# Two-layer transformer on one core: second layer's turn placed behind the q/k projection, other PSUM banks for second heads, and a last stage that alternates by head

## The chip, the cores and the metric

The kernel runs on one core of one Trainium2 chip. The metric is the device time of one execution in microseconds; lower is better. Before the change it is 988.21 us (median of 3 runs, 987.48 to 988.67).

## The reference

Eight sequences (B = 8) of 256 tokens with 256 features pass through two layers. Layer 0 has 16 attention heads of 128 dimensions with a causal mask, beside a feed-forward block in fp8. Layer 1 has 16 heads of 16 dimensions without a mask, beside a gated feed-forward block with Hadamard transforms.

```python
x = L0_attn_query                      # (8, 256, 256)
xn = _layernorm(x)
x = x + attn0(xn) + ffn0(xn)           # 16 heads x 128, causal, f32; fp8 feed-forward
xn = _layernorm(x)
x = x + attn1(xn) + ffn1(xn)           # 16 heads x 16, no mask; silu(gate) * up, then down
# attention: softmax(q @ k.T * scale) @ v, then @ w_o + b_o
```

## The kernel before, in words

Every f32 product is made of three bf16 products. A value is split into a high part (ScalarE copies PSUM to bf16) and a low part (VectorE subtracts the high part from PSUM). So nearly each PSUM tile is read first by ScalarE (`..._high`, line 807 or 808) and then by VectorE (`..._low`, line 812 or 813), and its bank is free only after both. There are eight banks: BK_QK, BK_M, BK_S, BK_O, BK_X, BK_VU, BK_S1, BK_Y.

The work is a software pipeline of steps s, written out as one list for each engine. The engines keep to their lists in order and meet through semaphores. The first stage of the kernel (layer 0's feed-forward, to about 110 us) is not touched. In steps 0 to 127 (NG0 = 128) a step does, on PE: `scores0(s-1)` (layer 0's scores, bank BK_S), the layer-1 scores of the head that belongs to the step (`scores1`, BK_S1), the q/k projection `proj_qk0(s)` (BK_QK), `turn0(s-2)` (the transposes of layer 0's softmax weights, BK_S again), `project_out0(s-4)` (BK_X), `turn1` (the transposes of the layer-1 weights of the head of step s-1, BK_O), then `proj_v0` in even steps or `up_gate` in odd ones (BK_VU), at some steps layer-1 pieces (`transpose_x1`, `proj_qkv1`, `attend1`: BK_M; `down`, `project_out1`: BK_Y), and last `attend0(s-3)` (BK_O). These names are functions of the kernel. Most matmuls are recorded at line 819 (the helper `group`); others have their own lines: `turn0` 841, `turn1` 869, `scores1` 902, `project_out0` 941, `attend1` 953, `transpose_x1` 965, `attend0` 1040 and 1042, `down` 1058, `project_out1` 1069. On the other engines: `max_0` 1321, `max_1` 1328 and the reciprocals 1350 and 1354 on VectorE; both exponentials 1162 and `gate_tanh` 1238 on ScalarE; `hidden` 1399 to 1406 on VectorE; the normalisations 1552 and 1559 and `hidden_low` 1564 on GpSimd.

A layer-1 sequence b starts 16 (b + 1) steps in (`start1`). Its heads lie one to a step from step 28 to 123 (sequences 0 to 5). The seventh sequence (b = 6) puts most of its 16 heads two to a step, into steps 124 to 132, and the eighth (LASTB = 7), which has no layer-0 work beside it, puts two into each of the steps from END = 134 to 141. The second head of a step is told by `second(n)`. Before, its scores go to BK_M and its turned weights to BK_S1. `x1_sum`, the layer norm, `transpose_x1(7)` and `proj_qkv1` (BK_S, BK_O, BK_X for the eighth sequence) lie in steps 131 to 133.

The waits that matter here: `turn1` into BK_O waits until `o0_low(s-4)` has emptied that bank; `attend0(s-3)`, which writes BK_O too, waits for `p1_low` of the head just turned and for `p0_low` of its own; `scores0(s)` at the start of the next step waits for `qk0_low(s)` and for `p0_low(s-2)`, since it writes BK_S. ScalarE's list of a step is `o0_high`, `exp_0`, `o1_high`, `qk0_high`, `p0_high`, `p1_high`, `exp_1`, then `v0_high` or `gate_tanh`. VectorE's is `max_0`, `o0_low`, `max_1`, `o1_low`, the reciprocal, `qk0_low`, `p0_low`, `p1_low`, second heads' `max_1`, `rec_1`, then `v0_low` or `hidden`. For steps from 134 on there is a shorter list for each engine. No DMA and no list of the DMA queue changes.

Of the kernel before, what the change touches and what calls it, by code (L numbers as in the profile page):

```python
# [18 lines left out]
def build(nc, t):  # L19
# [17 lines left out]
    with ExitStack() as ctx:  # L37
# [649 lines left out]
        def score1_bank(n):  # L687
            b, h = divmod(n, H1)
            if b == LASTB:
                return (BK_S1, BK_S)[h % 2]  # L690
            return BK_M if second(n) else BK_S1

        def turn1_bank(n):

            if n < LASTB * H1:
                return BK_S1 if second(n) else BK_O
            if n % 2 == 0:
                return BK_O
            return BK_X if head_slot(n) + 1 < END + 3 else BK_Y

        def second(n):

            return n > 0 and head_slot(n) == head_slot(n - 1)
# [112 lines left out]
        def pe_program(pe):  # L816
# [28 lines left out]
            def turn1(n):  # L845
                bank, slot = turn1_bank(n), head_slot(n) + 1
                if n < B * H1 - 1:
                    pe.wait_ge(norm1, n + 1)
                else:
                    pe.wait_ge(norm_last, 1)  # L850
                before = [m for m in range(n) if turn1_bank(m) == bank]
                if before:
                    pe.wait_ge(p1_lo, before[-1] + 1)
                if bank == BK_QK:
                    pe.wait_ge(qk0_lo, min(slot + 1, NG0))
                elif bank == BK_S1:
                    pe.wait_ge(exp1, 1 + max(m for m in range(B * H1)
                                             if score1_bank(m) == BK_S1 and head_slot(m) <= slot))
                elif bank == BK_X or bank == BK_O and n >= LASTB * H1:
                    pe.wait_ge(qkv1_lo, 3 * B)  # L860
                elif bank == BK_O:
                    pe.wait_ge(o0_lo, min(slot - 3, NG0))
                    if slot >= piece_slot(3 * LASTB):
                        pe.wait_ge(qkv1_lo, 3 * LASTB + 2)
                else:
                    pe.wait_ge(y_done, LASTB)
                for k in range(TT):
                    for i in range(TT):
                        last = nc.tensor.transpose(ps[:, bank, k * T + i * P:k * T + (i + 1) * P],  # L869
                                                   p1_of(n)[:, i, k * P:(k + 1) * P], ident[:, :])  # L870
                last.then_inc(p1_ps, 1)

            def scores1(n):
# [16 lines left out]
                    pe.wait_ge(p1_lo, turned[-1] + 1)  # L890
                if bank == BK_M:
                    free_m(pe, 0, n)
                if b == LASTB:
                    m, r = divmod(h // 2, 4)
                    rows32 = slice(32 * r, 32 * r + 32)
                    for i in range(TT):
                        last = group(ps[:, bank, i * T:(i + 1) * T],
                                     [(qm[rows32, h % 2, a, m, i * P:(i + 1) * P], qk1[rows32, c, 1, m, :])
                                      for a, c in PARTS])
                else:  # L900
                    for i in range(TT):
                        last = nc.tensor.matmul(ps[:, bank, i * T:(i + 1) * T],  # L902
                                                qs[:, h // 2, h % 2, i * P:(i + 1) * P],
                                                ks[:, b % 2, h // 2, :], start=True, stop=True)
                last.then_inc(s1_ps, 1)

            def proj_qk0(n):
                b, g = divmod(n, H0)
                if n == 0:
                    pe.wait_ge(xT_lo, PAIRS)  # L910
                if g == 0 and b >= 2:
                    pe.wait_ge(cur_ready[b % 2], 16 * (b // 2))
                if b == 0 and g % 4 == 0:
                    weights_ready(pe, ("qk", g // 4))
                for w in range(2):
                    last = group(ps[:, BK_QK, w * T:(w + 1) * T],
                                 [(wqkv0[:, a, w, k, g * HD0:(g + 1) * HD0], cur[:, b % 2, c, k, :])
                                  for k in range(KD) for a, c in PARTS])
                last.then_inc(qk0_ps, 1)
# [176 lines left out]
            for s in range(END):  # L1096
# [13 lines left out]
                for n in heads_in[s]:  # L1110
                    if second(n):
                        scores1(n)
                if 0 <= s - 2 < NG0:
                    turn0(s - 2)
                if 0 <= s - 4 < NG0:
                    project_out0(s - 4)
                for n in heads_in[s - 1]:
                    if not second(n):
                        turn1(n)
                if v_in(s) is not None:  # L1120
                    proj_v0(v_in(s))
                for n in hidden_in[s]:
# [20 lines left out]
                    pe_linear0(pe, PAIRS - 1, s - 4)  # L1143

            for s in range(END, y_slot(LASTB)):
                for n in heads_in[s]:
                    scores1(n)
                for n in heads_in[s - 1]:
                    turn1(n)
                for n in hidden_in[s]:  # L1150
                    up_gate(n, s)
                for n in downs_in[s]:
                    down(n)
                for n in outs_in[s]:
                    project_out1(n)
                for n in quads_in[s]:
                    attend1(n)

        def act_program(act):
# [91 lines left out]
            for s in range(END):  # L1251
# [9 lines left out]
                    exp_0(s - 1)  # L1261
                for n in quads_in[s - 1]:
                    o1_high(n)
                if s < NG0:
                    qk0_high(s)
                if 0 <= s - 2 < NG0:
                    p0_high(s - 2)
                for c in splits_in[s]:
                    split_high(act, c, 0)
                for n in heads_in[s - 1]:  # L1270
                    if not second(n):
                        p1_high(n)
                for n in heads_in[s]:
                    exp_1(n)
                if v_in(s) is not None:
# [19 lines left out]
            for s in range(END, y_slot(LASTB)):  # L1295
                for n in quads_in[s - 1]:
                    o1_high(n)
                for n in hidden_in[s - 1]:
                    gate_tanh(n)
                for e in range(2):  # L1300
                    for n in heads_in[s - 1][e:e + 1]:
                        p1_high(n)
                    for n in heads_in[s][e:e + 1]:
                        exp_1(n)

        def dve_program(dve):
            def o0_low(n):
# [153 lines left out]
            for s in range(END):  # L1461
# [27 lines left out]
                        o1_low(n)  # L1489
                if 0 <= s - 1 < NG0:  # L1490
                    rec_0(s - 1)
                if s < NG0:
                    qk0_low(s)
                if 0 <= s - 2 < NG0:
                    p0_low(s - 2)
                for n in heads_in[s - 1]:
                    if not second(n):
                        p1_low(n)
                fold(s)
                for n in heads_in[s]:  # L1500
                    if second(n):
# [27 lines left out]
            for s in range(END, y_slot(LASTB) + 1):  # L1529
                for n in quads_in[s - 1]:  # L1530
                    o1_low(n)
                for e in range(2):
                    for n in heads_in[s][e:e + 1]:
                        max_1(n)
                    for n in heads_in[s - 1][e:e + 1]:
                        p1_low(n)
                    if e == 0:
                        for n in hidden_in[s - 1]:
                            hidden(n)
                    for n in heads_in[s][e:e + 1]:  # L1540
                        rec_1(n)
                if B * H1 - 1 in heads_in[s]:
                    norm_1(B * H1 - 1)
                for b in y_in[s]:
# [246 lines left out]
```

## Time and profile before

| what | value |
|---|---|
| median of 3 runs | 988.21 us |
| the profiled execution | 989.46 us |
| its span, first to last instruction | 987.5 us |
| mean granted TensorE clock | 0.978 |
| PE busy | 905.1 us (92%) |
| VectorE busy | 753.9 us (76%) |
| ScalarE busy | 680.5 us (69%) |
| GpSimd busy | 347.0 us (35%) |

Span is the time from the first to the last instruction of the program in that one execution. Busy time is the union of an engine's instructions. Matmuls overlap each other, so PE's busy time includes the tail of each; start-to-start distances tell better what PE does in a step. A wait is put down to the instruction that released it last.

### The profile page before, as it was taken

What the parts mean: (1) busy time and instruction counts of PE and PEld (TensorE: products, weight loads), DVE (VectorE), ACT (ScalarE), POOL (GpSimd) and SP (SyncE); (2) the same over time, 40 slices, a digit from 0 to 9 for tenths busy, and PEclk for the clock granted to TensorE, in tenths of its full rate; (3) what the DMA queues carried; (4) which work ended last, traced back from release to release, by engine and by line L of the source; (5) the groups of instructions that cost most, each with busy time, mean ns of one, the idle gap of its engine ahead of it and who ended that gap; (6) DMA issues with size and microseconds to landing.
All of it is one profiled execution on the core that took longest, in us unless ns stands there. A gap on an engine that the chain in (4) does not pass through costs nothing.

```text
span 987.5 us, 22866 instructions
## 1 busy us (share of the span) xinstructions
PE 905.1 (92%) x8032; PEld 724.6 (73%) x8032; DVE 753.9 (76%) x2128; ACT 680.5 (69%) x1997; POOL 347.0 (35%) x637
## 2 busy tenths in 40 slices
PE   4786889899999999999999999999999999886887
PEld 2344667677788788887888788888888888765665
DVE  6886677667887888888888878788888888766466
ACT  4786786557767776777677777777677767755454
POOL 5502456424333333333333333333333333333242
PEclk9998999999999999999999999999999999989799
DMA  9243260002000100010002000200020001000000
GB/s 309 78 150 96 91 209 2 2 22 60 2 2 23 48 23 2 23 50 23 1 3 70 1 23 2 66 7 23 2 62 10 23 2 39 22 23 1 2 12 12
DMA packets 46880, 39.98 MB, mean 40 GB/s; under 512 B 4400, under 2 KB 42032, under 8 KB 46512
## 3 DMA queue, kind: packets, MB, share of 16 engines
q1 hardware_dynamic: 46768, 38.52, 12.7%
q8 instruction: 66, 1.08, 0.5%
q14 instruction: 46, 0.38, 0.1%
HBM read 30.11 MB, written 8.39 MB: 39 GB/s over the span
## 4 chain that ended last, share of the span: by engine, by line
PE 60%; DVE 18%; ACT 10%; issue 4%; ACTq 0%; DVEq 0%
PE ps L819 32%; PE ps L941 6%; ACT arena L1162 5%; DVE arena L812 5%; PE ps L869 5%; DVE arena L813 4%; PE ps L1040 3%; PE ps L1058 3%; PE ps L841 3%; ACT arena L808 3%; DVE arena L1321 3%; PE ps L902 2%; ACT arena L807 2%; PE ps L1069 2%; PE ps L1042 1%
## 5 line engine op out<-in xcount | busy, mean ns | idle before, releaser
L813 DVE SCALAR_TENSOR_TENSOR arena<-ps,bqk,arena 128x256 bf16<-128x256 f32 x416 | 187.5, 480 | 77.0 <-ACT arena L808 77.0
L808 ACT ACTIVATE arena<-ps,bqk 128x256 bf16<-128x256 f32 x416 | 177.8, 463 | 82.4 <-PE ps L1042 64.0
L812 DVE TENSOR_TENSOR arena<-ps,arena 128x512 bf16<-128x512 f32 (+1 forms) x336 | 204.4, 633 | 35.3 <-ACT arena L807 35.0
L819 PE MATMUL ps<-arena,wqkv 128*128 128x256 bf16 x1728 | 216.9, 276 | 0.3 <-DVE arena L812 0.3
L807 ACT ACTIVATE arena<-ps 128x512 bf16<-128x512 f32 (+1 forms) x336 | 181.0, 558 | 47.6 <-PE ps L869 30.3
L1552 POOL TENSOR_SCALAR arena<-arena,rc 128x128 f32<-128x128 f32 (+1 forms) x256 | 105.5, 425 | 273.2 <-DVE rc L1350 273.1
L1162 ACT ACTIVATE arena<-arena,nb 128x128 f32<-128x128 f32 (+1 forms) x256 | 114.4, 447 | 126.3 <-DVE nb L1321 126.2
L1559 POOL TENSOR_SCALAR arena<-arena,rc 128x256 f32<-128x256 f32 x254 | 118.2, 478 | 232.1 <-DVE rc L1354 232.1
L819 PEld LDWEIGHTS ps<-arena,wqkv 128*128 128x128 bf16 x1728 | 171.5, 99 | 24.5 <-issue 0.8
L1162 ACT ACTIVATE arena<-ps,nb 128x256 f32<-128x256 f32 x256 | 119.3, 478 | 16.3 <-DVE nb L1328 16.3
L819 PE MATMUL ps<-arena 128*128 128x128 bf16 (+2 forms) x864 | 98.4, 251 | 16.7 <-DVE arena L813 6.5
L941 PE MATMUL ps<-wo,arena 128*128 128x256 bf16 x768 | 105.4, 274 | 0.9 <-DVE arena L813 0.9
L819 PE MATMUL ps<-wqkv,arena 128*128 128x512 bf16 (+1 forms) x480 | 105.7, 359 | 0.0
L1321 DVE CUSTOM_DVE_ANT_0 arena<-ps,mask 128x128 f32<-128x128 f32 (+1 forms) x256 | 81.0, 354 | 31.2 <-PE ps L819 30.9
L819 PE MATMUL ps<-arena,wug 128*128 128x256 bf16 x768 | 95.6, 275 | 0.0
L1328 DVE TENSOR_REDUCE nb<-ps 128x2 f32<-128x512 f32 x128 | 87.1, 680 | 0.5 <-PE ps L819 0.4
L869 PE MATMUL ps<-ident,arena 128*128 128x128 f32 x512 | 78.4, 279 | 9.3 <-ACT arena L1162 7.2
L819 PEld LDWEIGHTS ps<-arena,wug 128*128 128x128 bf16 x768 | 75.7, 99 | 8.8 <-issue 0.2
L941 PEld LDWEIGHTS ps<-wo,arena 128*128 128x128 bf16 x768 | 74.4, 98 | 10.0 <-DVE arena L813 1.1
L819 PEld LDWEIGHTS ps<-arena 128*128 128x128 bf16 (+1 forms) x864 | 62.4, 98 | 26.3 <-DVE arena L813 14.8
L869 PEld LDWEIGHTS ps<-ident,arena 128*128 128x128 f32 x512 | 60.2, 143 | 15.1 <-issue 11.6
L819 PEld LDWEIGHTS ps<-wqkv,arena 128*128 128x128 bf16 x480 | 47.2, 98 | 32.7 <-issue 0.8
(115 smaller groups left out, 1283.6 us busy)
## 6 DMA issues: line engine op xcount, KB each, us to landing
scratch_qk<-arena SPq DMA_DIRECT2D x28, 128.0 KB, 1.9
arena<-scratch_qk SPq DMA_DIRECT2D x84, 32.0 KB, 1.8
arena<-scratch_qk SPq DMA_DIRECT2D x42, 64.0 KB, 2.5
arena<-in_x SPq DMA_DIRECT2D x4, 512.0 KB, 9.7
arena<-in_w_gating SPq DMA_DIRECT2D x4, 512.0 KB, 7.7
arena<-in_w_q SPq DMA_DIRECT2D x4, 512.0 KB, 4.6
arena<-in_w_k SPq DMA_DIRECT2D x4, 512.0 KB, 5.6
arena<-in_w_v SPq DMA_DIRECT2D x2, 1024.0 KB, 6.5
```

The costliest lines, as they stand in the source:

```text
L807: return nc.scalar.activation(out, in_, ACT.Copy)
L808: return nc.scalar.activation(out, in_, ACT.Identity, bias=bias)
L812: return nc.vector.tensor_tensor(out, in_, hi, ALU.subtract)
L813: return nc.vector.scalar_tensor_tensor(out=out, in0=in_, scalar=bias, in1=hi, op0=ALU.add, op1=ALU.subtract)
L819: last = nc.tensor.matmul(out, lhsT, rhs, start=(n == 0), stop=(n == len(steps) - 1))
L869: last = nc.tensor.transpose(ps[:, bank, k * T + i * P:k * T + (i + 1) * P], p1_of(n)[:, i, k * P:(k + 1) * P], ident[:, :])
L941: last = nc.tensor.matmul(ps[:, BK_X, i * D:(i + 1) * D], oT0[:, a, n % 2, i * P:(i + 1) * P], wo0[:, c, h, :], start=False, stop=(h == H0 ...
L1162: last = nc.scalar.activation(outs[i], ins[i], ACT.Exp, bias=bias[:, i:i + 1], scale=scale, accum_out=sums[:, i:i + 1])
L1321: last = nc.vector.tensor_tensor_reduce(out=sp0[:, n % 3, a:z], in0=ps[:, BK_S, a:z], in1=mask[:, a:z], scale=-SCALE0, scalar=3.0e38, op0= ...
L1328: nc.vector.tensor_reduce(nb1[:, n % 4, :], ps[:, score1_bank(n), :].rearrange("p (i k) -> p i k", i=TT), AX.X, ALU.max, negate=True).then ...
L1552: last = nc.gpsimd.tensor_scalar(v, v, rc0[:, n % 4, i:i + 1], 1.0, ALU.mult, ALU.mult)
L1559: last = nc.gpsimd.tensor_scalar(v, v, rc1[:, n % 4, i:i + 1], 1.0, ALU.mult, ALU.mult)
```

## The change

Three things change, with no instruction added or removed.

1. `turn1` of a step's first head comes directly behind `proj_qk0` (and a second head's scores), ahead of `turn0` and `project_out0`, on PE; `p1_high` stands ahead of `qk0_high` on ScalarE; `p1_low` ahead of `qk0_low` and `p0_low` on VectorE.
2. Second heads use other banks. Scores go to BK_M in steps up to 127 and to BK_QK from 128. Turned weights go to BK_QK in steps up to 127 and to BK_S from 129. The waits follow the banks; `proj_qk0` gains one, for a turn in BK_QK.
3. In steps from 134 on PE does the first head's scores and turn, `up_gate`, and then the second head's scores and turn. ScalarE's `gate_tanh` and VectorE's `hidden` lie between the two heads.

```diff
@@ score1_bank, turn1_bank
-            return BK_M if second(n) else BK_S1
+            if second(n):
+                return BK_M if head_slot(n) < NG0 else BK_QK
+            return BK_S1
...
-                return BK_S1 if second(n) else BK_O
+                if second(n):
+                    return BK_QK if head_slot(n) + 1 < NG0 else BK_S
+                return BK_O
@@ turn1, scores1, proj_qk0: waits
-                elif bank == BK_S1:
-                    pe.wait_ge(exp1, 1 + max(m for m in range(B * H1)
-                                             if score1_bank(m) == BK_S1 and head_slot(m) <= slot))
+                elif bank == BK_S:
+                    pe.wait_ge(p0_lo, NG0)
...
+                if bank == BK_QK:
+                    pe.wait_ge(qk0_lo, NG0)
...
+                turned = [m for m in range(B * H1) if turn1_bank(m) == BK_QK and head_slot(m) + 1 < n]
+                if turned:
+                    pe.wait_ge(p1_lo, turned[-1] + 1)
@@ PE, steps below END
+                for n in heads_in[s - 1]:
+                    if not second(n):
+                        turn1(n)
                 if 0 <= s - 2 < NG0:
                     turn0(s - 2)
                 if 0 <= s - 4 < NG0:
                     project_out0(s - 4)
-                for n in heads_in[s - 1]:
-                    if not second(n):
-                        turn1(n)
@@ PE, steps from END
-                for n in heads_in[s]:
-                    scores1(n)
-                for n in heads_in[s - 1]:
-                    turn1(n)
-                for n in hidden_in[s]:
-                    up_gate(n, s)
+                for e in range(2):
+                    for n in heads_in[s][e:e + 1]:
+                        scores1(n)
+                    for n in heads_in[s - 1][e:e + 1]:
+                        turn1(n)
+                    if e == 0:
+                        for n in hidden_in[s]:
+                            up_gate(n, s)
@@ ScalarE, steps below END
+                for n in heads_in[s - 1]:
+                    if not second(n):
+                        p1_high(n)
                 if s < NG0:
                     qk0_high(s)
                 if 0 <= s - 2 < NG0:
                     p0_high(s - 2)
                 for c in splits_in[s]:
                     split_high(act, c, 0)
-                for n in heads_in[s - 1]:
-                    if not second(n):
-                        p1_high(n)
@@ ScalarE, steps from END
-                for n in hidden_in[s - 1]:
-                    gate_tanh(n)
                 for e in range(2):
                     for n in heads_in[s - 1][e:e + 1]:
                         p1_high(n)
                     for n in heads_in[s][e:e + 1]:
                         exp_1(n)
+                    if e == 0:
+                        for n in hidden_in[s - 1]:
+                            gate_tanh(n)
@@ VectorE, steps below END
+                for n in heads_in[s - 1]:
+                    if not second(n):
+                        p1_low(n)
                 if s < NG0:
                     qk0_low(s)
                 if 0 <= s - 2 < NG0:
                     p0_low(s - 2)
-                for n in heads_in[s - 1]:
-                    if not second(n):
-                        p1_low(n)
@@ VectorE, steps from END
                     for n in heads_in[s - 1][e:e + 1]:
                         p1_low(n)
+                    for n in heads_in[s][e:e + 1]:
+                        rec_1(n)
                     if e == 0:
                         for n in hidden_in[s - 1]:
                             hidden(n)
-                    for n in heads_in[s][e:e + 1]:
-                        rec_1(n)
```

## Rows read from the trace of the kernel before

**Rows 1.** Busy time by stretch, two of fifty us: PE, PEld, DVE, ACT, POOL, then PEclk, DMA share, GB/s

```profile
500.00:550.00 50.00, 49.22 (x468) 41.41 (x467) 40.03 (x114) 36.99 (x115) 16.53 (x36) 1.00 0.13 36
...
850.00:900.00 50.00, 40.54 (x348) 31.83 (x344) 34.19 (x95) 32.61 (x104) 17.17 (x37) 0.93 0.04 12
```

**Rows 2.** Waits of PE from 250 to 850 us: us in total, times, longest

```profile
PE ps L1040 <- DVE arena L812: 6.8, 18, 0.5
PE ps L841 <- DVE nb L1321: 2.7, 6, 0.5
```

**Rows 3.** Timeline of step 92, and the same `attend0` one round (16 steps) later

```profile
646.90 0.48 DVE L813 SCALAR_TENSOR_TENSOR arena<-ps,bqk,arena 128x256 bf16<-128x256 f32 x1
...
647.43 0.49 PE L841 MATMUL ps<-ident,arena 128*128 128x128 f32 x3
...
648.41 0.60 PE L869 MATMUL ps<-ident,arena 128*128 128x128 f32 x4
648.62 1.02 ACT L807 ACTIVATE arena<-ps 128x384 bf16<-128x384 f32 x2
...
648.76 0.88 DVE L813 SCALAR_TENSOR_TENSOR arena<-ps,bqk,arena 128x256 bf16<-128x256 f32 x2 [0.56 <-ACT arena L808]
...
649.55 1.15 DVE L812 TENSOR_TENSOR arena<-ps,arena 128x384 bf16<-128x384 f32 x2
...
650.84 0.49 PE L1040 MATMUL ps<-arena 128*128 128x256 bf16 x3 [0.53 <-DVE arena L812]
...
651.33 0.33 PE L819 MATMUL ps<-arena 128*128 128x128 bf16 x3
...
753.05 0.49 PE L1040 MATMUL ps<-arena 128*128 128x256 bf16 x3 [0.53 <-DVE arena L812]
```

**Rows 4.** Waits of PE from 850 us to the end: us in total, times, longest

```profile
PE ps L869 <- ACT arena L1162: 7.2, 7, 3.4
PE ps L819 <- ACT arena L1162: 3.5, 5, 1.7
PE ps L902 <- DVE arena L812: 3.3, 4, 1.8
PE ps L902 <- DVE arena L813: 3.0, 2, 2.1
```

**Rows 5.** Timeline of steps 128 to 133, where PE waits longest

```profile
885.66 0.58 PE L902 MATMUL ps<-arena 128*128 128x256 bf16 x2 [2.08 <-DVE arena L813]
...
913.86 1.09 PE L869 MATMUL ps<-ident,arena 128*128 128x128 f32 x4 [3.36 <-ACT arena L1162]
...
920.37 1.08 PE L869 MATMUL ps<-ident,arena 128*128 128x128 f32 x4 [1.69 <-ACT arena L1162]
...
923.07 0.80 PE L819 MATMUL ps<-arena,wqkv 128*128 128x256 bf16 x3 [0.34 <-DVE arena L812]
```

**Rows 6.** Busy time of one stretch, columns as in the first group

```profile
912.80:926.40 13.60, 10.39 (x46) 7.28 (x47) 5.70 (x12) 5.70 (x18) 3.52 (x8) 0.50 0.01 1
```

**Rows 7.** Timeline of one round of the last sequence (steps 140 and 141)

```profile
966.75 0.82 PE L819 MATMUL ps<-arena 32*128 32x256 bf16 x6 [0.50 <-ACT arena L1162]
...
967.50 1.12 PE L869 MATMUL ps<-ident,arena 128*128 128x128 f32 x8
...
969.43 0.41 DVE L1399 SCALAR_TENSOR_TENSOR arena<-arena,ps 128x256 f32<-128x256 f32 x1
...
970.62 0.67 DVE L1328 TENSOR_REDUCE nb<-ps 128x2 f32<-128x512 f32 x1
...
971.32 0.47 ACT L1162 ACTIVATE arena<-ps,nb 128x256 f32<-128x256 f32 x1 [1.13 <-DVE nb L1328]
...
972.24 0.38 ACT L1238 ACTIVATE arena<-ps 128x256 f32<-128x256 f32 x1
...
972.40 0.82 PE L819 MATMUL ps<-arena 32*128 32x256 bf16 x6 [0.40 <-ACT arena L1162]
```

## The prediction

> **What bounds the kernel now.** I read four views in this order: busy time by stretch, the waits of PE, the timeline of a step, and the timeline of the end. The stretch from 500 to 550 us has PE busy for 49.2 of 50 us at the full granted clock (1.00, the 2.4 GHz level); from 850 us it falls to 40.5 of 50 [rows 1]. So up to step 123 PE is the bound, and behind it nobody is. In 250 to 850 us PE's named waits are only 6.8 us ahead of `attend0` (L1040) and 2.7 us ahead of `turn0` (L841) [rows 2]. These rows understate a little, since a matmul's own tail counts as busy; counted from start to start I find about 2.75 us lost in each 16 steps. One round of 16 steps is 753.05 - 650.84 = 102.2 us (the same `attend0` of two rounds) [rows 3].
>
> The last two sequences are different: between 850 us and the end PE waits 7.2 us ahead of `turn1` (L869) for an exponential, and 3.3 and 3.0 us ahead of `scores1` (L902) for VectorE's conversions, besides 3.5 us ahead of the last sequence's scores [rows 4]. Nearly all of these are waits for a PSUM bank, not for data.
>
> **The middle (steps 28 to 123, six rounds).** `turn1` moves ahead of `turn0` and `project_out0`; `p1_high` and `p1_low` move ahead of the q/k and p0 conversions. No instruction is added. Take the step whose rows are shown [rows 3]. Before, `turn1` starts at 648.41, ScalarE's copy ends at 649.64, but `p1_low` stands behind `p0_low` and ends at 649.55 + 1.15 = 650.70; `attend0`, which writes the same bank, starts 0.14 us after that. That 0.14 is the hand-off VectorE to PE. The bank BK_O is also why the moved `turn1` gets a new neighbour: it needs `o0_low`, which ends at 646.90 + 0.48 = 647.38, so it can start at 647.52, not at 647.43 where `turn0` starts now. From there: 1.23 us to the end of the copy (648.41 to 649.64), 0.03 and 0.69 for `p1_low`: 649.47, 1.2 us earlier, and the wait at `attend0` is gone.
>
> What is late next: the q/k and p0 conversions. They end about 3.3 us after `turn1`'s start (1.23 for the copy, about 0.8 for ScalarE's q/k pair, 0.88 for VectorE's [rows 3], 0.5 for p0, less overlaps), so at 650.83, and the next step's `scores0`, which reuses BK_S, can start at 650.97. Before it starts at 651.33 [rows 3]: 0.36 us won. But ScalarE now waits for `turn1` early, and behind that wait stand its q/k, p0, exp, v and tanh work, behind `p1_low` those of VectorE: the last conversions of a step end 0.1 to 0.2 us later (an estimate from the same rows); VectorE begins the next step late, `o0_low` is late, and the new `turn1` stands right behind it. Going so through the 16 positions of a round, I win 0.37, 0.32, 0.13 and 0.14 us (positions 12, 15, 14, 10, counted as step number modulo 16) and lose 0.43, 0.09, 0.08, 0.07, 0.04 (positions 0, 4, 13, 9, 5); the rest have no wait before or after. Sum -0.25 us a round, **-1.5 us** for six. Bounds: all waits go, -2.75 x 6 = -16 us; or the positions that lose do so twice as much and those that win do not, +0.7 x 2 x 6 = +8 us. I take -1.5 as the one worked out from the rows, nearer the middle of the two.
>
> The Trainium skill ("Trainium Kernel Development and Optimization", Performance Expectations) says that matmul busy time is a bad metric because matmuls are pipelined. By it the round has more to give than the busy rows show; my count from start to start agrees in direction, 2.75 us a round against 1.6 (9.5 us of named waits in some six rounds). The sum above already uses the larger figure as its bound; by the smaller one the bound would be -9.5.
>
> **Steps 124 to 133, two heads a step.** Here the second head's turn wrote BK_S1, so it waited for this step's exponential and held up the next step's scores; its scores wrote BK_M, which the quads and pieces of the second layer use. The change puts turns into BK_QK (steps 125 to 127) and BK_S (from 129), and scores into BK_QK from step 128.
> - Steps 124 to 127: scores still use BK_M, and the turn in BK_QK now needs this step's `qk0_low` and holds up the next `proj_qk0` until `p1_low`. That comes out at the same time as before within 0.1 us twice. About -0.2 us in all.
> - Step 128: PE waits 2.08 us before 885.66 for `o1_low` (BK_M) [rows 5]. In BK_QK it only needs the last `p1_low`, about 883.2. With `turn1` early, VectorE's second maximum comes some 2.9 us earlier; step 129 starts 3.3 us earlier.
> - Steps 129 to 131: `scores1` no longer waits for a turn in BK_S1 (the wait of at most 1.8 us in [rows 4]); now `o0_low` behind `hidden` is what turn1 waits for. Gain grows to 4.5 us at `x1_sum`.
> - Steps 131 and 132: the waits of 3.36 us before 913.86 and of 1.69 us before 920.37 [rows 5] are for an exponential of the same bank. In BK_S they go; what remains is VectorE's and GpSimd's own chain (layer norm, maximum, reciprocal, norm, turn). The last sequence's q projection, now at 923.07 [rows 5], starts about 6.9 us earlier.
> The ceiling is the three bank waits, 7.2 + 3.3 + 3.0 = 13.5 us; the floor is nothing, if VectorE's chain holds all. I take **-6.9**, about half, the value of the walk.
>
> **The end (steps 134 to 141).** The scores are K = 32 rows and each step's two heads went in pairs. A round now is 972.40 - 966.75 = 5.65 us [rows 7]: scores of the odd head, the turns at 967.50 behind them, copy, `p1_low`, the hidden conversion 969.43 to 970.62, the odd maximum, the exponential at 971.32, and 1.08 us later the next odd scores. After the change the even turn does not stand behind the odd scores, so that ring is cut. The next ring is on VectorE and ScalarE: maximum 0.67, exponential with hand-off 1.08 less 0.1, tanh 0.38, hidden with reciprocal 1.19, maximum 0.67, exponential 0.98, reciprocal 0.15: 5.0 us. PE's own work in a step is about 4.8, so it is close behind. Six rounds at 0.6 are 3.6; the first step and the drain add about 0.4: **-4.0 us**, bounds 0 (if ScalarE's new order, tanh behind the even exponential, holds `hidden` up) and -5.6 (PE's 4.8 alone, with the first step).
>
> **The clock.** From 912.8 to 926.4 us the granted clock is 0.50, the 1.2 GHz level, after a stretch in which PE was idle for 3.36 us in one piece [rows 5, 6]; the q/k/v projection of the last sequence runs in it at half speed. I keep it as it is: even after the change PE waits there for the layer norm. If it vanished, some 3 us more would go. The Trainium skill ("TensorE: Matmul & The Clock Gate", HAM oscillation) says idle gaps bring the half rate and sustained work lifts it; by that rule the shorter gaps could give back these 3 us. The trace agrees so far that the low level follows idle PE.
>
> **Sum.** -1.5 - 0.2 - 6.9 - 4.0 = -12.6, and the -0.2 is already within the -6.9, so -12.4. The profiled execution took 989.46 us (span 987.5), 1.25 above the median of 988.21; against the median the result is 988.21 - 12.4 = **975.8 us**.
>
> **The rivals.**
> - *The middle wins all of its waits*: the ring over VectorE is shorter than I reckon and PE runs without a gap. -16 - 11 = -27: 961 us. For: the rows show hand-offs of 0.14 only. Against: five of 16 positions start VectorE late already. 0.07.
> - *The tail's banks were not the bound*: layer norm, maxima and conversions take the time the bank waits had; 6.9 becomes 2, and the end gives 2. 988.2 - 5.5 = 982.7. For: VectorE is busy in much of it. Against: in both large waits the exponential waited for is followed by nothing that PE needs but the bank. 0.14.
> - *Slower, by `turn1` behind `o0_low`*: place: the middle, 96 steps. The margin is small: `o0_low` ends 0.05 us ahead of the projection's successor in [rows 3] and 0.3 in most steps, the hand-off costs 0.14. If VectorE's later end carries over, each step grows, and all three engines run in one ring. At 0.2 us a step this is +19 - 11 = +8: 996 us. It decides at 11 / 96 = 0.115 us a step; my walk has five positions beyond this, but not the mean. 0.09.
> - *The clock returns* (above): 972.5. 0.06.
> - *No difference*, middle and tail cancelling within 2 us: 0.03.
> Nothing in the order of semaphores keeps the change from doing what it says.
>
> **How the numbers follow.** The forecast has 0.61. Its own range is 970 to 981 from the bounds of its terms (the middle -5 to +3, the tail 2 either way). The range for 8 in 10 reaches to the rival at 982.7 and the clock's, so 966 to 984.5; outside remain the two extreme rivals and no change. A measurement tells about 0.2%, 2 us. Faster: 0.61 + 0.07 + 0.14 + 0.06 = 0.88. Same 0.03. Slower 0.09.
>
> **What would show it.** In the middle: no wait left ahead of L1040, new waits ahead of L869 (for L813) and of the first L819 of a step (for L812), a round of 102.0. At step 128 no wait for `o1_low`; the q projection of the last sequence at about 915 us; rounds of 5.0 at the end. Wrong would be: a round above 103 or below 100 us, or the last exponentials still 5.6 us apart.

## The result: 0.5% faster, a third of the forecast gain

| | before | after |
|---|---|---|
| median | 988.40 us (6 runs, 987.30 to 989.13) | 984.14 us (6 runs, 982.89 to 985.07) |
| profiled execution, span | 989.46, 987.5 us | 984.19, 982.1 us |
| mean granted clock | 0.978 | 0.984 |

The ratio is 0.9949, its 95% interval 0.9933 to 0.9964. Forecast were 975.8 us, -12.4; measured are -4.3 in the medians and -5.4 in the spans. The time lies inside the stated range, at its upper end.

I took the two timelines apart at the same six places in each: the first `scores0` of steps 26 and 124, the last sequence's q projection, its first scores (head 112), its last exponential (head 127) and the final result; the last two stages stand together below. Differences of those start times:

| stage, us | before | after | change | forecast |
|---|---|---|---|---|
| start to step 26 | 226.7 | 228.0 | +1.3 | 0 |
| steps 26 to 123 | 623.15 | 625.12 | +1.97 | -1.5 |
| step 124 to the last q projection | 73.23 | 66.62 | -6.6 | -6.9 |
| that projection to the first scores | 8.2 | 8.9 | +0.6 | 0 |
| the end, with its drain | 53.0 | 50.3 | -2.7 | -4.0 |

**Steady state.** Waits of PE from 250 to 850 us in the changed kernel, which answer to [rows 2].

```profile
PE ps L872 <- DVE arena L817: 10.2, 19, 0.8
```

Busy time in the stretches of [rows 1], columns as there.

```profile
500.00:550.00 50.00, 49.43 (x468) 42.09 (x470) 40.62 (x117) 36.96 (x115) 15.90 (x34) 1.00 0.13 36
...
850.00:900.00 50.00, 40.89 (x380) 33.18 (x380) 36.98 (x103) 34.69 (x112) 18.08 (x39) 1.00 0.04 13
```

The 6.8 us ahead of `attend0` are gone, as forecast, and so are the 2.7 ahead of `turn0`. In their place is a single wait: `turn1` (L872 now) for `o0_low` (a conversion at L817), 10.2 us in 19 waits. The waits were swapped for one of about the same total, 10.2 us for 9.5. PE's busy share says nothing about that: it rose from 49.22 to 49.43 of 50 us while the middle got longer. The second wait that I had named, of a step's first `scores0` for L816, is not in the view.

**Step 80, the worst of each round (position 0).** The timeline of PE and VectorE in the kernel before:

```profile
566.87 0.66 PE L819 MATMUL ps<-arena 128*128 128x128 bf16 x6
566.98 0.41 DVE L1399 SCALAR_TENSOR_TENSOR arena<-arena,ps 128x256 f32<-128x256 f32 x1
...
568.64 0.48 DVE L813 SCALAR_TENSOR_TENSOR arena<-ps,bqk,arena 128x256 bf16<-128x256 f32 x1
...
568.90 0.49 PE L841 MATMUL ps<-ident,arena 128*128 128x128 f32 x3
...
571.61 0.38 PE L823 MATMUL ps<-brow,ones 128*128 128x512 bf16 x1
571.83 0.82 PE L1058 MATMUL ps<-wdn,arena 128*128 128x256 bf16 x6
```

And the same step in the changed kernel:

```profile
568.49 0.66 PE L823 MATMUL ps<-arena 128*128 128x128 bf16 x6
...
569.01 0.41 DVE L1410 SCALAR_TENSOR_TENSOR arena<-arena,ps 128x256 f32<-128x256 f32 x1
...
570.33 0.42 DVE L1332 CUSTOM_DVE_ANT_0 arena<-ps,mask 128x256 f32<-128x256 f32 x1
...
570.67 0.48 DVE L817 SCALAR_TENSOR_TENSOR arena<-ps,bqk,arena 128x256 bf16<-128x256 f32 x1
...
571.29 0.63 PE L872 MATMUL ps<-ident,arena 128*128 128x128 f32 x4 [0.63 <-DVE arena L817]
571.76 0.49 PE L845 MATMUL ps<-ident,arena 128*128 128x128 f32 x3
571.96 0.60 ACT L811 ACTIVATE arena<-ps 128x512 bf16<-128x512 f32 x1 [0.18 <-PE ps L872]
```

Count from the step's first `scores0`. PE reached its turn 2.03 us in (568.90 - 566.87) and `o0_low` ended 2.25 us in; that cost nothing, because `turn0`, which came first, does not wait for it. Now VectorE starts its `hidden` work 0.52 us in instead of 0.11, `o0_low` ends 2.66 us in, and `turn1`, which does use BK_O, stands there until 2.80. `turn0` stands behind it. It needs only `max_0`, whose second half (L1332) ended at 570.33 + 0.42 = 570.75, and with the 0.14 us that VectorE to PE took in [rows 3] it could have started 2.40 us in. So two things come together here: everything on VectorE is late, and `turn1` is at the head of the list. The out projection is no loser of its own, since it waits for the same `o0_low`.

**The tail and its clock.** The timeline of PE in steps 128 to 132 of the changed kernel, which answers to [rows 5].

```profile
886.63 0.38 PE L907 MATMUL ps<-arena 128*128 128x256 bf16 x2 [0.39 <-issue]
...
912.57 0.66 PE L973 MATMUL ps<-ident,arena 128*128 128x128 f32 x4 [2.53 <-DVE arena L1441]
...
914.87 2.29 PE L872 MATMUL ps<-ident,arena 128*128 128x128 f32 x8 [1.43 <-POOL arena L1570]
...
919.70 0.58 PE L823 MATMUL ps<-arena,wqkv 128*128 128x256 bf16 x2 [1.25 <-DVE arena L816]
```

Busy time of the stretch that answers to [rows 6].

```profile
913.70:923.90 10.20, 7.69 (x34) 5.25 (x35) 4.17 (x11) 4.94 (x14) 2.81 (x6) 0.52 0.01 2
```

The waits of 2.08, 3.36 and 1.69 us are gone. What is left are waits for the layer norm (L1441) and GpSimd's norm (L1570), and ahead of them `turn1` behind `o0_low` again, as forecast for steps 129 to 131 (L872 for L817 in the view below, 6.9 us from step 124 on). Behind the 2.53 us of idle PE the granted clock is again at its 1.2 GHz level (0.52).

**The end.** Waits of PE from 850 us on in the changed kernel, which answer to [rows 4].

```profile
PE ps L872 <- DVE arena L817: 6.9, 6, 1.8
PE ps L823 <- DVE arena L816: 2.6, 2, 1.3
PE ps L973 <- DVE arena L1441: 2.5, 1, 2.5
PE ps L872 <- DVE arena L1346: 2.1, 1, 2.1
```

Timeline of one round of the last sequence, which answers to [rows 7].

```profile
960.87 0.47 ACT L1172 ACTIVATE arena<-ps,nb 128x256 f32<-128x256 f32 x1 [1.38 <-DVE nb L1339]
961.79 0.47 ACT L812 ACTIVATE arena<-ps,bv 128x256 bf16<-128x256 f32 x1
962.29 0.48 DVE L817 SCALAR_TENSOR_TENSOR arena<-ps,bv,arena 128x256 bf16<-128x256 f32 x1 [0.20 <-ACT arena L812]
962.69 0.68 DVE L1339 TENSOR_REDUCE nb<-ps 128x2 f32<-128x512 f32 x1
...
966.58 0.47 ACT L1172 ACTIVATE arena<-ps,nb 128x256 f32<-128x256 f32 x1 [1.38 <-DVE nb L1339]
```

In the last four rounds odd exponentials come 5.0 and 5.7 us apart by turns. The 5.71 (960.87 to 966.58) is a step with `o1_high` (L812) and `o1_low` (L817), which stand first in the lists. All seven distances between the odd exponentials of the last sequence:

| into step | 135 | 136 | 137 | 138 | 139 | 140 | 141 |
|---|---|---|---|---|---|---|---|
| before | 7.14 | 5.65 | 5.65 | 6.87 | 5.65 | 5.65 | 5.65 |
| after | 6.89 | 5.31 | 5.65 | 5.70 | 5.01 | 5.71 | 5.00 |

The 6.87 stands out. Up to its start the kernel before ran at the 1.2 GHz level for 3.4 us, and one `up_gate` (the matmuls from wug) took 2.73 us instead of 1.47. PE's timeline, and busy time of the stretch with columns as in [rows 1]:

```profile
948.58 0.82 PE L819 MATMUL ps<-arena 32*128 32x256 bf16 x6 [1.71 <-ACT arena L1162]
...
950.29 2.73 PE L819 MATMUL ps<-arena,wug 128*128 128x256 bf16 x12
...
957.13 1.47 PE L819 MATMUL ps<-arena,wug 128*128 128x256 bf16 x12
```

```profile
950.30:953.70 3.40, 3.40 (x18) 2.25 (x16) 2.97 (x7) 2.27 (x9) 1.02 (x3) 0.50 0.25 80
```

The changed kernel has no such stretch between its last sequence's first scores and last exponential. So of the 2.7 us won at the end some 1.2 (6.87 - 5.65) come with the clock and some 1.4 with the order; this is an estimate from the distances above, since every profile with the old end has the stretch.

### The profile page after: what moved, and what is told of

Read it like the earlier page. It is cut to its first block, busy times and chain, and to the rows that moved or that the text cites. A ratio compares the mean times of both kernels' runs of the same rounds, so it can differ in the third digit from the quotient of the medians.

```text
span 982.1 us, 22791 instructions
## 1 busy us (share of the span) xinstructions
PE 895.5 (91%) x7965; PEld 722.1 (74%) x8032; DVE 761.7 (78%) x2128; ACT 682.9 (70%) x1997; POOL 348.3 (35%) x637
## 4 chain that ended last, share of the span: by engine, by line
PE 64%; DVE 17%; ACT 7%; issue 5%; POOL 0%; another core or an unknown queue 0%; ACTq 0%; DVEq 0%; POOLq 0%
PE ps L823 34%; PE ps L949 6%; PE ps L872 6%; DVE arena L817 4%; PE ps L1066 3%; PE ps L845 3%; PE ps L1048 3%; ACT arena L1172 3%; ACT arena L812 3%; DVE arena L816 3%; DVE arena L1332 2%; PE ps L1077 2%; PE ps L907 2%; PE ps L961 2%; PE ps L1050 1%
## 5 line engine op out<-in xcount | busy, mean ns | idle before, releaser
L816 DVE TENSOR_TENSOR arena<-ps,arena 128x512 bf16<-128x512 f32 (+1 forms) x336 | 212.7, 636 | 74.9 <-ACT arena L811 74.2
L812 ACT ACTIVATE arena<-ps,bqk 128x256 bf16<-128x256 f32 x416 | 179.9, 472 | 66.1 <-PE ps L1050 49.5
L823 PE MATMUL ps<-arena,wqkv 128*128 128x256 bf16 x1728 | 216.8, 276 | 2.7 <-DVE arena L816 2.6
L811 ACT ACTIVATE arena<-ps 128x512 bf16<-128x512 f32 (+1 forms) x336 | 187.9, 564 | 43.3 <-PE ps L872 29.8
L817 DVE SCALAR_TENSOR_TENSOR arena<-ps,bqk,arena 128x256 bf16<-128x256 f32 x416 | 187.5, 479 | 34.0 <-ACT arena L812 30.1
L1570 POOL TENSOR_SCALAR arena<-arena,rc 128x256 f32<-128x256 f32 x254 | 119.0, 482 | 232.1 <-DVE rc L1365 232.1
L823 PEld LDWEIGHTS ps<-arena,wqkv 128*128 128x128 bf16 x1728 | 171.2, 99 | 27.1 <-DVE arena L816 2.0
L823 PE MATMUL ps<-arena 128*128 128x128 bf16 (+2 forms) x864 | 98.3, 250 | 14.7 <-DVE arena L817 6.5
L872 PE MATMUL ps<-ident,arena 128*128 128x128 f32 x512 | 80.0, 279 | 21.8 <-DVE arena L817 17.1
L1332 DVE CUSTOM_DVE_ANT_0 arena<-ps,mask 128x128 f32<-128x128 f32 (+1 forms) x256 | 80.8, 353 | 24.1 <-PE ps L823 23.4
L823 PE MATMUL ps<-wqkv,arena 128*128 128x512 bf16 (+1 forms) x425 | 94.0, 357 | 2.8
L823 PE MATMUL ps<-arena,wug 128*128 128x256 bf16 x768 | 94.3, 273 | 0.0
L872 PEld LDWEIGHTS ps<-ident,arena 128*128 128x128 f32 x512 | 56.9, 142 | 37.6 <-issue 26.9
L823 PEld LDWEIGHTS ps<-arena,wug 128*128 128x128 bf16 x768 | 75.1, 98 | 8.8 <-issue 0.2
L823 PEld LDWEIGHTS ps<-arena 128*128 128x128 bf16 (+1 forms) x864 | 61.5, 98 | 26.3 <-DVE arena L817 14.8
L823 PEld LDWEIGHTS ps<-wqkv,arena 128*128 128x128 bf16 x480 | 47.2, 98 | 33.3 <-issue 1.0
```

Source lines behind the costliest of these rows:

```text
L811: return nc.scalar.activation(out, in_, ACT.Copy)
L812: return nc.scalar.activation(out, in_, ACT.Identity, bias=bias)
L816: return nc.vector.tensor_tensor(out, in_, hi, ALU.subtract)
L817: return nc.vector.scalar_tensor_tensor(out=out, in0=in_, scalar=bias, in1=hi, op0=ALU.add, op1=ALU.subtract)
L823: last = nc.tensor.matmul(out, lhsT, rhs, start=(n == 0), stop=(n == len(steps) - 1))
L1332: last = nc.vector.tensor_tensor_reduce(out=sp0[:, n % 3, a:z], in0=ps[:, BK_S, a:z], in1=mask[:, a:z], scale=-SCALE0, scalar=3.0e38, op0= ...
```

## The experiments

Runs that were sent together share the runs of the kernel before on their chip: 988.58 us (27 runs) for e1 to e4, 988.12 (17 runs) for e5, e6, e9 and e11, and 991.65 (11 runs, 987.96 to 992.63) for e7, e12 and e13. The ratio is what compares across these groups.

**e1, the middle alone.** The new order of `turn1` and p1 in steps below 124; banks and end as before.

```diff
+        EARLY = lambda s: s < 124
                 for n in heads_in[s - 1]:
-                    if not second(n):
+                    if not second(n) and EARLY(s):
                         turn1(n)
                 ...
+                for n in heads_in[s - 1]:
+                    if not second(n) and not EARLY(s):
+                        turn1(n)
```

(the same around `p1_high` and `p1_low`)

> Only part 1, and only in steps below 124; banks and the last stage are as before. Theory A (turn1 now stands behind o0_low, and the steps that start late pay more than the removed waits at attend0 give): about 2 us slower than before, a round of 16 steps of 102.55 us instead of 102.22, the loss in positions 0, 4, 5 and 9, waits ahead of L869 for L813 in their place. Rival B (the middle is neutral or better, and the missing gain of the changed kernel is elsewhere, for instance in its first 230 us, where its profile is 1.3 us late): 0 to 1.5 us faster, and a start of step 26 at 226.7 us as before.

Measured: 990.00 us, 12 runs, ratio 1.0021 (1.0009 to 1.0033). Steps 26 to 123 take 625.11 us against 623.15. PE's waits of 250 to 850 us:

```profile
PE ps L870 <- DVE arena L814: 10.2, 19, 0.8
```

That is the same wait as in the changed kernel. The reordering by itself makes the kernel slower, by 2.0 us in the middle; the sign of my term was wrong.

**e2, the banks alone.** The hunks of `score1_bank`, `turn1_bank` and their waits; all lists as before.

> Only part 2 (banks of the second heads); order and last stage as before. Theory A (the bank waits of steps 124 to 133 carry the gain of this stage, and the order is needed for about a third of it): the last sequence's q projection starts 4 to 5 us earlier, 4 to 5 us faster in all. Rival B (the bank waits are covered by VectorE's chain unless turn1 comes early): at most 2 us faster.

Measured: 983.01 us, 10 runs (977.60 to 986.34), ratio 0.9943 (0.9923 to 0.9963); the profiled execution was the slowest of these. Step 124 to the last q projection takes 65.96 us, no more than with the early turns on top (66.62). So the banks carry the gain of that stage without the order. The middle is as before, 623.14 us, and so are PE's waits of 250 to 850 us:

```profile
PE ps L1048 <- DVE arena L816: 7.3, 19, 0.5
PE ps L845 <- DVE nb L1329: 2.7, 6, 0.5
```

**e3, the end alone.** The hunks of the lists from END on PE, ScalarE and VectorE.

> Only part 3 (the last stage alternates by head). Theory A: from the start of the last sequence's scores to the end 2.5 to 3 us are saved, rounds of 5.0 us without and 5.7 us with an o1 conversion, about 2.7 us faster in all. Rival B (half of what the changed kernel gains here is the half-clock stretch at 950 us, which it misses by chance of its timing): 1.2 to 1.5 us faster.

Measured: 987.29 us, 12 runs, ratio 0.9983 (0.9968 to 0.9997). The stage from the first scores of the last sequence to its last exponential takes 43.02 us instead of 45.69, as in the changed kernel (43.03). That is theory A's size, but it doesn't rule out rival B: e3 misses the half-clock stretch of the end too, while e1 and e2, with the old end, have it at the same place (19.0 and 19.3 us behind their first scores, 19.0 before) and take 45.69 us as well. The whole run gained less than the stage, 0.3 to 3.2 us by its interval.

The three parts add up within their intervals, which are 1 to 2 us wide either way: +2.1 - 5.6 - 1.7 = -5.2 us by their ratios, against -5.0 by the ratio of the whole change (0.0051 x 988).

**e4, the change without its middle.** e1's edit with `EARLY = lambda s: s >= 124` on the changed kernel.

> The changed kernel with the old order in steps below 124, the new one from 124. Theory A (the middle costs 2 us): 2 us faster than the changed kernel, 6.3 us faster than the kernel before (982.1). Rival B (the middle costs nothing): the same as the changed kernel, 4.3 us faster than before (984.1).

Measured: 981.46 us, 6 runs, ratio 0.9933 (0.9917 to 0.9950); the middle is back at 623.05 us. The interval of the ratio overlaps that of the whole change, so it is the stage that tells: with e1 it shows from both sides that the middle costs 2 us. PE's waits of 250 to 850 us are those of before:

```profile
PE ps L1049 <- DVE arena L817: 7.2, 19, 0.5
PE ps L846 <- DVE nb L1339: 2.7, 6, 0.5
```

**e5, o1's conversions out of the ring.** The changed kernel, with `o1_high` and `o1_low` behind the first head's p1 conversion in the steps from END.

```diff
-                for n in quads_in[s - 1]:
-                    o1_high(n)
                 for e in range(2):
                     for n in heads_in[s - 1][e:e + 1]:
                         p1_high(n)
+                    if e == 0:
+                        for n in quads_in[s - 1]:
+                            o1_high(n)
```

(and so for `o1_low`, behind `p1_low`)

> The changed kernel; in the last stage the o1 conversions of both engines move from the front of a step to behind the first head's p1 conversion, where both engines wait 0.3 to 0.5 us. Theory A (a round of the last stage is a ring over VectorE and ScalarE, and the o1 conversions lie in it in every other round): the rounds of 5.7 us become 5.0 to 5.2, three of them, 1.5 to 2 us faster than the changed kernel. Rival B (PE's own work of 5.0 us and project_out1 bound those rounds): 0 to 0.3 us.

Measured: 982.62 us, 6 runs, ratio 0.9941 (0.9925 to 0.9957). The last sequence's stage shrinks from 43.03 to 41.71 us. The intervals of e5 and of the change overlap, so the gain stands by the timeline of the end, where a round with o1 now takes 5.01 us:

```profile
960.64 0.47 ACT L1172 ACTIVATE arena<-ps,nb 128x256 f32<-128x256 f32 x1 [1.12 <-DVE nb L1340]
...
965.65 0.47 ACT L1172 ACTIVATE arena<-ps,nb 128x256 f32<-128x256 f32 x1 [0.92 <-DVE nb L1340]
```

**e6, the order by position.** The changed kernel with the old order where the new one loses: e1's edit with `EARLY = lambda s: not (s < 124 and s % 16 in (0, 4, 5, 9))`.

> The changed kernel with the old order of turn1 and the p1 conversions in positions 0, 4, 5 and 9 of each 16 steps, where it loses. Theory A (each position's loss is its own turn1 standing behind o0_low): a round of about 101.9 us instead of 102.55, about 3.5 us faster than the changed kernel. Rival B (the loss is carried in from the steps before, whose conversions end later, and only shows there): at most 1 us faster, a round above 102.3.

Measured: 979.63 us, 6 runs, ratio 0.9912 (0.9893 to 0.9930). The middle takes 619.96 us, 5.2 less than with the new order in all positions and 3.2 less than before. PE's waits of 250 to 850 us:

```profile
PE ps L846 <- DVE nb L1339: 3.3, 11, 0.4
PE ps L1049 <- DVE arena L817: 1.4, 6, 0.2
PE ps L873 <- DVE arena L818: 0.2, 1, 0.2
```

4.9 us of waits instead of 10.2 (and of 9.5 in [rows 2]): each order is right in some steps, and wrong in others. By position, against the kernel before, the old order takes back all of the loss in 5 and 9 (0.13 and 0.10 us) and turns 0.21 in position 4 into a gain of 0.10. In position 0 it takes back only 0.30 of 0.72. In step 80 of e6 `hidden` again starts 0.52 us in, and `turn0`, now first, waits 0.23 us for `max_0` and starts 2.41 us in instead of 2.03. So 0.42 us of that position's loss are carried in by the steps before, as rival B said, and only 0.30 are `turn1` behind `o0_low`.

**e9, `o0_low` first.** If the wait is for `o0_low`, put it ahead of `max_0` in VectorE's list.

```diff
-                if 0 <= s - 1 < NG0:
-                    max_0(s - 1)
                 if 0 <= s - 4 < NG0:
                     o0_low(s - 4)
+                if 0 <= s - 1 < NG0:
+                    max_0(s - 1)
```

> The changed kernel with o0_low ahead of max_0 in VectorE's list, and nothing else. Theory A (the new turn1 waits for o0_low, which waits behind max_0): the 10.2 us of waits ahead of L872 from 250 to 850 us fall below 2, max_0 comes 0.15 us later and costs nothing since ScalarE waits for turn1 anyway; a round of 101.0 to 101.5 us instead of 102.55, 6 to 9 us faster than the changed kernel. Rival B (the ring is VectorE's work as a whole, o0_low only its visible member): the waits move to another place, the round stays above 102.2, at most 2 us faster.

Measured: 989.18 us, 12 runs (986.61 to 991.27), ratio 1.0010 (0.9999 to 1.0022). The wait of `turn1` fell to 1.2 us, and another took its place, ahead of L823, for the conversions of L816 (PE's waits of 250 to 850 us):

```profile
PE ps L823 <- DVE arena L816: 5.4, 18, 0.6
PE ps L872 <- DVE arena L817: 1.2, 6, 0.2
```

The middle is 1.2 us shorter than in the changed kernel (623.96). But `o0_low` itself waits for ScalarE's `o0_high`; in the steps compared `max_0` started 1.11 instead of 0.70 us into the step, where I had assumed 0.15 more, and everything behind the first exponential is later. The start to step 26, which this edit touches too, took 233.6 us, beyond the 226.5 to 230.6 of the kernels that are alike there. That start, and not the middle, makes the kernel slower than the changed one.

**e11, the same with the old order.** e9's edit, and `turn1` and p1 at their old places everywhere; banks and end as changed.

> Banks and last stage as changed, old order of turn1 everywhere, and o0_low ahead of max_0. Theory A: the swap pays only because turn1 stands behind o0_low; with the old order nothing on PE wants o0_low early, turn0 gets max_0 later, so the round is 102.2 to 102.8 us and the kernel 0 to 3 us slower than without the swap (981.5, the run with all but the middle). Rival B (the swap is good for VectorE by itself): the same gain as in the changed kernel, 5 us or more.

Measured: 1004.45 us, 4 runs, ratio 1.0162 (1.0148 to 1.0176), and 640.35 us in the middle. I had expected nothing of this size on either theory. Two waits grew, that of `attend0` from 6.8 to 15.6 us and that of `turn0` from 2.7 to 6.4 (PE, 250 to 850 us):

```profile
PE ps L1048 <- DVE arena L816: 15.6, 28, 0.8
PE ps L845 <- DVE nb L1332: 6.4, 11, 0.8
```

So the swap costs 17.2 us in the middle behind the old order, where in the new one it gains 1.2. These named waits grew by 12.5 us; I did not trace the rest, and that the late `max_0` is the cause of all of it is not shown.

**e13, `turn0` ahead of `turn1`.** The changed kernel, with these two swapped on PE only.

```diff
+                if 0 <= s - 2 < NG0:
+                    turn0(s - 2)
                 for n in heads_in[s - 1]:
                     if not second(n):
                         turn1(n)
-                if 0 <= s - 2 < NG0:
-                    turn0(s - 2)
```

> The changed kernel with turn0 ahead of turn1 on PE alone (turn1 still ahead of project_out0; the lists of ScalarE and VectorE as changed). Theory A (what the changed kernel loses is PE standing idle for o0_low with turn0 ready behind it): the waits ahead of L872 fall from 10.2 us to about 4, but all conversions come 0.33 us later, so positions 12 and 15 lose 0.2 to 0.3 us each; a round of 102.1 to 102.4 us, 1 to 2.5 us faster than the changed kernel. Rival B (the early conversions carry all of the gain): the round grows beyond 102.55 us, slower than the changed kernel.

Measured: 984.79 us, 6 runs, ratio 0.9940 (0.9919 to 0.9961); the middle takes 623.92 us. `turn1`'s wait is gone, and two others stand in its place (PE, 250 to 850 us):

```profile
PE ps L823 <- DVE arena L816: 5.6, 13, 0.4
PE ps L845 <- DVE nb L1332: 5.3, 11, 0.7
```

In e9 and here the waits went elsewhere: 10.2 us in one place, 6.6 and 10.9 in others. The sum of named waits is no measure of the length either: here it is larger than in the changed kernel, and the middle is 1.2 us shorter. As a whole the run can't be told from the changed kernel (984.79 and 984.14 us): the stage behind step 124 took 67.60 us, 1.0 more.

**e7, e6 and e5 together.**

> The order by position and the o1 conversions moved, both at once. Theory: the two lie in different stages and add, 4.5 + 1.5 = 6 us faster than the changed kernel, about 978.1 us. Rival (the end of the program hides part of it, or the granted clock falls more often once PE waits less evenly): 979.5 us or more.

Measured: 977.01 us, 4 runs (975.27 to 978.58), ratio 0.9860 (0.9837 to 0.9884); stages 620.08 us in the middle, 41.70 in the last sequence. It beats both kernels. Its group's runs of the kernel before were some 3 us longer than those of the other groups, so the ratio flatters it a little; against 988.4 it is 1.15% faster.

**e12, e7 with the old order from step 124 on as well.** `EARLY = lambda s: s < 124 and s % 16 not in (0, 4, 5, 9)`.

> As the run before, but from step 124 the old order of turn1 and the p1 conversions. Theory A (the gain of steps 124 to 133 is the banks', the early turn1 gives nothing there; the run with the banks alone took 66.0 us from step 124 to the last q projection, the changed kernel 66.6): the same stretch is 66.0 us, 0 to 0.7 us faster than the run before. Rival B (the walk of the prediction: the early turn1 carries a third of this stage's gain once the last stage alternates too): 2 us slower or more.

Measured: 977.31 us, 4 runs, ratio 0.9863 (0.9842 to 0.9884): no difference from e7. In steps 124 to 133 the early turn is worth nothing either way (67.03 and 66.63 us, and 6.58 and 7.92 in the projections behind).

## Why the prediction was right and wrong

**The middle, -1.5 forecast, +2.0 measured: the step that failed.** The mechanism of the walk was right, `turn1` behind `o0_low`, and so was the list of who wins and loses; the sizes tipped the sum. Mean change of a step by position, over four rounds in the middle (steps 44 to 107), from `scores0` to `scores0`:

| position | 12 | 15 | 14 | 10 | 0 | 4 | 5 | 9 | 13 |
|---|---|---|---|---|---|---|---|---|---|
| forecast | -0.37 | -0.32 | -0.13 | -0.14 | +0.43 | +0.09 | +0.04 | +0.07 | +0.08 |
| measured | -0.30 | -0.29 | -0.17 | -0.17 | +0.72 | +0.21 | +0.13 | +0.10 | +0.08 |

The rest are 0.00, as forecast. The wins came to -0.93 of -0.96, the losses to +1.24 of +0.71: +0.32 us a round instead of -0.25, and 102.54 us a round, not the 102.0 that I named. The term that failed is the 0.71 us of losses; they measured 1.24. Position 0 makes half of the error, 0.29 us. There PE opens BK_Y for the down projection with a matmul that takes 0.22 us (571.61 to 571.83 in step 80 before); my walk of the changed step left it out. The recorded text gives only the 0.43 us, and no run shows that this piece is what was missing. In positions 4, 5 and 9 the losses were sized 0.03 to 0.12 us too small; which part of VectorE's late start makes this stays open. The range's bound for the middle (-5 to +3) held it. e6 shows that the list by position was worth acting on: with the old order where it loses, the middle gains 3.2 us.

**Steps 124 to 133, -6.9 forecast, -6.6 measured.** At step 128 the wait for `o1_low` is gone, and the q projection came at 919.70, not at the 915 that I named (923.07 - 6.9 - 1.5 = 914.7): it carries the 3.5 us missed in the middle, 1.3 from the start and 0.3 of its own stage. The term is met in size, but partly by luck. e1 and e3, whose banks are those of before, need only 71.19 and 71.72 us for this stage, where the profiled execution of before needed 73.23. In that one PE ran at the 1.2 GHz level in two short stretches (busy time, columns as in [rows 1]):

```profile
865.00:868.00 3.00, 3.00 (x19) 2.16 (x18) 2.57 (x9) 1.38 (x6) 0.80 (x2) 0.50 0.01 3
...
885.50:889.00 3.50, 3.33 (x17) 2.83 (x18) 1.24 (x4) 0.49 (x1) 0.83 (x2) 0.52 0.00 0
```

e1 has neither of them, e3 only the second. Matched matmul by matmul from step 128 on, before falls 1.5 us behind e1 in the second stretch; steps 125 and 126, around the first, are 0.5 us longer than in e1. Together that is the difference of 2.0 us. Against e1 the banks are worth 4.6 to 5.2 us, 1.7 to 2.3 less than forecast, and the forecast had no clock in it. And only the banks: e2 and e12 show that the early turn, which I counted in at step 128 ("VectorE's second maximum comes some 2.9 us earlier"), brings nothing.

**The end, -4.0 forecast, -2.7 measured.** Of the 2.7 us some 1.2 are the half-clock stretch that fell away (an estimate, see the result), so the new order gave some 1.4 of the 4.0 forecast. A round of 5.0 us, as worked out for the ring of VectorE and ScalarE, came only into steps 139 and 141. I had summed the ring over a step without `o1_high` and `o1_low`; every second step has them, first in both lists, and takes 0.7 us more. e5 moved them out: 5.0 in those rounds too, 1.3 us gained. The round into step 137 stays at 5.65 us in all of these kernels, and why is open. PE's own work was undersized as well, at 4.8 us a step: in e5 it runs without a named wait from 954.83 to 965.33 us, two steps, so 5.2 to 5.3 us each, and a faster ring alone would soon meet it.

**What had no term.** The start to step 26 was 1.3 us longer and the last projections 0.6. The start is not the change's: e1 to e4 are alike there, and took 228.0 to 230.6 us. I had no term for it, and yet it is 1.3 of the 7.0 us by which the span missed the forecast; the others are 3.5 (middle), 1.3 (end), 0.6 and 0.3.

**The rivals.** *Slower by `turn1` behind `o0_low`* had the right mechanism and far too high a price: I gave it 0.2 us a step and a deciding point of 0.115; measured are 1.97 / 98 = 0.02. It has eaten some 2 us of the 6.6 that e4 shows without it, not all. *The middle wins all of its waits* fell: the waits moved. *The banks not the bound* fell in its mechanism (e2), though its time, 982.7, was nearer than mine. *No difference* fell: the interval of the ratio ends at 0.9964. *The clock returns* fell for its own stretch: 0.52 after PE was idle for 2.53 us. The Trainium skill ("TensorE: Matmul & The Clock Gate", HAM oscillation) says that idle gaps bring the half rate; by that rule, the trace agrees in direction: shorter gaps were still gaps. Elsewhere, where I had no term, some 3.2 us did come back: the 2.0 in steps 124 to 133 and the estimated 1.2 at the end.

## What to carry to other kernels

Moving an instruction ahead in an in-order list trades the wait behind it for a wait ahead of it: find what the moved one needs, who produces that, and how late this producer is in each step of the round, and if the margins differ by step, let the order differ too (e6: -3.2 us where the same order everywhere gave +2.0). A round that differs every second time must be walked twice, and before a stage's gain is put down to an edit, the granted clock of that stage must be compared in both kernels. A bank that two users share is a bound of its own, and giving each its own bank needed no reordering at all.

## What the hardware showed

Stretches at the 1.2 GHz level do not fall at the same place in kernels with the same work there. e3 and e2 ran on the same chip and are alike in the first 120 us. From 30 to 60 us e3 was granted 0.89 (busy time of the stretch, columns as in [rows 1]):

```profile
30.00:60.00 30.00, 22.62 (x118) 12.39 (x117) 25.55 (x48) 23.93 (x41) 8.62 (x8) 0.89 0.26 80
```

The same stretch in e2, at 0.77:

```profile
30.00:60.00 30.00, 22.94 (x101) 11.92 (x100) 23.07 (x43) 22.17 (x38) 9.16 (x8) 0.77 0.21 63
```

Step 26 began at 228.0 us in e3 and at 230.6 in e2, and at 226.7 in before. The waits of PE alone don't tell where such a stretch falls. In step 125 PE is idle for 1.22 us in the kernel before and in e3 alike (to 864.0 us and to 865.2); the kernel before drops to 0.50 at 865.0 and e3 stays at 1.00. Ahead of the second layer's scores of step 128 PE is idle for 2.08 us in the kernel before and in e1 alike; the kernel before drops there (0.52) and e1 does not. The stretch in the last sequence is the regular one here: the three profiles with the old end (before, e1, e2) have PE idle for 1.7 us and then the low level, and the ten with the new end have neither between that sequence's first scores and its last exponential.

A part that is worth 2 us is therefore to be read from its own stage, and with the clock of that stage beside it: a single span can be off by more.
